# Three PSUM banks re-dealt, half-width projections and an earlier transpose in the first phase of a two-layer kernel

## The reference

```python
x1 = layernorm(x)                                    # folded with the next line into one scale and shift
z = rmsnorm(x1, pre_norm_w) @ in_proj_w.T            # 256 -> 768 channels
z_pre = causal_depthwise_conv(z, short_w, taps=3) + short_b
x2, x1, v = split(z_pre, 3)                          # 256 channels each
xv = x1 * v
y = (long_conv(xv, h) + xv * D_skip) * x2            # h from 16 poles a channel
...                                                  # out projection, gated MLP, layernorm; then an FFN layer
```

## Time and profile before

| | |
|---|---|
| median of 3 runs | 1097.38 us (1095.71 to 1097.52) |
| the profiled execution | 1095.71 us, span 1093.9 us |
| phase A | 0 to about 189 us of the span |
| PE busy | 97% of the span |
| DVE, ACT, POOL busy | 80%, 66%, 27% |
| granted TensorE clock | 0.998 of full speed |

### The profile page before, as it was taken

The page is one execution under the profiler, slowest core; times in us unless marked ns, Lnnn a source line. Parts: engine busy times, 40 slices in busy tenths (PEclk is TensorE's granted clock), DMA queues, the critical chain, the costliest instruction groups (busy, mean ns, idle before and its releaser), DMA issues.

```text
span 1093.9 us, 25039 instructions
## 1 busy us (share of the span) xinstructions
PE 1063.1 (97%) x9016; PEld 1007.7 (92%) x9016; DVE 879.1 (80%) x2313; ACT 720.8 (66%) x1613; POOL 298.7 (27%) x577
## 2 busy tenths in 40 slices
PE   8899999999999999999999999989999999999996
PEld 7777787778999999999999999989999999999996
DVE  7999998763788877888888777898888888877874
ACT  7878887664565666666666666665666666666553
POOL 6677784620001111112111111121112111111111
PEclk9999999999999999999999999999999999999999
DMA  3338988984642333333333333443333333333100
GB/s 127 117 126 229 270 229 219 400 312 59 147 73 40 59 60 49 59 49 50 52 55 63 56 59 49 109 105 50 50 59 49 51 53 57 65 59 49 31 11 30
DMA packets 113051, 104.93 MB, mean 96 GB/s; under 512 B 7600, under 2 KB 103792, under 8 KB 112672
## 3 DMA queue, kind: packets, MB, share of 16 engines
q1 hardware_dynamic: 111696, 100.77, 42.1%
q0 software_dynamic: 736, 2.51, 0.7%
q10 hardware_dynamic: 496, 0.05, 0.0%
HBM read 77.84 MB, written 32.80 MB: 101 GB/s over the span
## 4 chain that ended last, share of the span: by engine, by line
PE 63%; DVE 7%; issue 4%; POOL 1%; ACT 1%; DMA 0%; ACTq 0%; SPq 0%; DVEq 0%; POOLq 0%
PE ps_ring L1464 33%; PE ps_w L1464 14%; PE ps_m L1464 9%; PE ps_o L1464 4%; PE ps_rt L1479 2%; DVE base L1318 1%; POOL sc L1082 1%; DVE bn L1222 1%; PE ps_m L1529 1%; DVE prod L1265 0%; PE ps_w L1474 0%; DMA base<-in_w 0%; DVE ht_l L1234 0%; DVE pt_l L1234 0%; DVE x L1436 0%
## 5 line engine op out<-in xcount | busy, mean ns | idle before, releaser
L1082 POOL TENSOR_TENSOR sc<-sc,neg_half 128x2 f32<-128x2 f32 x128 | 95.5, 746 | 690.6 <-DVE sc L1417 407.8
L1142 ACT ACTIVATE gate<-ps_ring 128x256 f32<-128x256 f32 x192 | 73.0, 381 | 127.4 <-PE ps_ring L1464 126.6
L1163 ACT ACTIVATE hid<-ps_ring,b1s 128x256 f32<-128x256 f32 x256 | 112.4, 484 | 29.4 <-PE ps_ring L1464 9.3
L1464 PE MATMUL ps_ring<-mt_h,wl_h 128*128 128x256 f32 x640 | 125.8, 278 | 2.4 <-DVE prod L1265 1.3
L1464 PE MATMUL ps_ring<-mt_l,wl_h 128*128 128x256 f32 x640 | 125.7, 278 | 2.2 <-DVE mt_l L1234 2.2
L1464 PE MATMUL ps_ring<-mt_h,wl_l 128*128 128x256 f32 x640 | 125.0, 277 | 0.0
L1234 DVE TENSOR_TENSOR ht_l<-hid,ht_h 128x256 fp32r<-128x256 f32 x256 | 103.1, 423 | 16.0 <-ACT ht_h L1167 10.0
L1464 PE MATMUL ps_ring<-xt_h,we_h 128*128 128x256 f32 x512 | 103.2, 283 | 2.8 <-DVE prod L1265 2.4
L1265 DVE TENSOR_TENSOR prod<-ps_ring,gate 128x256 f32<-128x256 f32 x192 | 80.7, 420 | 24.9 <-ACT gate L1142 20.6
L1464 PEld LDWEIGHTS ps_ring<-mt_h,wl_h 128*128 128x128 f32 x640 | 96.6, 188 | 3.9 <-ACT mt_h L1211 2.2
L1464 PE MATMUL ps_ring<-xt_h,we_l 128*128 128x256 f32 x512 | 99.9, 276 | 0.0
(11 more groups left out here) (186 smaller groups left out, 2746.6 us busy)
## 6 DMA issues: line engine op xcount, KB each, us to landing
toep_scratch<-taps_scratch SPq DMA_DIRECT2D x30, 512.0 KB, 7.7
toep<-toep_scratch SPq DMA_DIRECT2D x30, 512.0 KB, 9.9
xa<-in_x SPq DMA_DIRECT2D x16, 512.0 KB, 5.0
x_scratch<-x2c SPq DMA_DIRECT2D x16, 512.0 KB, 3.7
x2s<-x_scratch SPq DMA_DIRECT2D x32, 256.0 KB, 6.9
xa_c<-in_x SPq DMA_DIRECT2D x32, 256.0 KB, 2.7
xb_c<-in_x SPq DMA_DIRECT2D x32, 256.0 KB, 2.7
out<-frow SPq DMA_DIRECT2D x32, 256.0 KB, 2.9
```

Source lines behind the costliest of these rows:

```text
L1082: nc.gpsimd.tensor_tensor(sc[:, to], sc[:, to], neg_half[:, 0, 0:CC], ALU.pow).then_inc(S[done], 1)
L1142: nc.scalar.activation(gate[rows_of, m % 2], ring[m % RING][rows_of, 0], ACT.Gelu_apprx_tanh).then_inc(S["gate_done"], 1)
L1163: nc.scalar.activation(hid[:, m % HIDS], block_of, ACT.Gelu, bias=b1s[:, m:m + 1]).then_inc(S["hid_done"], 1)
L1464: mm = nc.tensor.matmul(out, lhs(a, kk), rhs(b, kk), start=(j == 0), stop=(closed and j == len(todo) - 1))
```

## The change

- The PSUM banks are dealt anew: one bank `ps_t` for transposed rows where there were two, and five slots of `ps_z` where there were four. In unit 0 the second half goes to `ps_x0`.
- `turn_rows(n+1, 0)` moves from behind position 1 to behind position 0. Each `turn_rows` waits for the `turned_low` just before it. `turned_high` and `turned_low` of half 0 move to position 0, and DVE's `measure` calls to 1, 2, 4, 5.
- `norm_rows` does one chunk at each of the positions 2, 3, 4 and 5.
- `project` writes each bank in two halves of 256 columns, with twelve matmuls where there were six.
- At the second sequence's start ScalarE writes the bias, as for unit 0, and no longer GpSimd.

```diff
-    OVER, SLOTS, XBUFS = TAPS - 1, 4, 3
+    HALF, OVER, SLOTS, XBUFS = TA // 2, TAPS - 1, 5, 3
-    NORMED = {2: (0,), 4: (1,), 5: (2, 3)}
...
-        ps_t = [ps(ctx, f"ps_t{b}", [P, TA]) for b in range(KB)]
+        ps_t = ps(ctx, "ps_t", [P, TA])
...
+        def turned_bank(u, b):
+
+            return ps_x[0][:].rearrange("p c t -> p (c t)") if (u, b) == (0, 1) else ps_t[:]
...
             def carry(u, j):
-                over = pair[:, :, TA:]
-                if opens(u + 1):
-                    biases = sbias[:, KB:].rearrange("p (a k) -> p k a", k=KB)[:, j]
-                    over = biases.unsqueeze(2).broadcast_to([P, KB, OVER])
-                nc.gpsimd.tensor_copy(pair[:, :, 0:OVER], over).then_inc(S["carried"], 1)
+                nc.gpsimd.tensor_copy(pair[:, :, 0:OVER], pair[:, :, TA:]).then_inc(S["carried"], 1)
...
             def first_tap(u, i):
-                if u == 0:
+                if opens(u):
                     nc.scalar.activation(sums(m, u)[:, 0:OVER], zero[:], ACT.Identity, scale=1.0,
...
         def _(act):
-                    if i in (1, 3) and valid(n + 1, UA):
+                    if i in (0, 3) and valid(n + 1, UA):
                         turned_high(n + 1, i // 3)
                     if i in (1, 3) and valid(n - 1, UA):
                         gate_rows(n - 1, i // 2)
-                    if i in NORMED and valid(n + 2, UA):
-                        norm_rows(n + 2, NORMED[i])
+                    if i >= 2 and valid(n + 2, UA):
+                        norm_rows(n + 2, (i - 2,))
...
         def _(dve):
-                        if n == 0:
-                            dve.wait_ge(S["opened"], i + 1)
+                        if opens(n):
+                            dve.wait_ge(S["opened"], ZB * (n * B // UA) + i + 1)
...
-                    if i in (1, 3):
+                    if i in (0, 3):
                         if valid(n + 1, UA):
                             turned_low(n + 1, i // 3)
                     elif valid(n + 3, UA):
-                        measure(n + 3, i // 2 if i < 3 else i - 2)
+                        measure(n + 3, i - 1 if i < 3 else i - 2)
...
         def _(pe):
             def turn_rows(u, b):
                 if u > 0:
-                    pe.wait_ge(S["zl_done"], KB * (u - 1) + b + 1)
+                    pe.wait_ge(S["zl_done"], KB * u + b)
...
             def project(u, i):
-                passes = [(w, r, k) for w, r in ((0, 0), (1, 0), (0, 1)) for k in range(KB)]
-                for j, (w, r, k) in enumerate(passes):
-                    mm = nc.tensor.matmul(slot(b)[:], win_r[w][:, k, m * P:(m + 1) * P], zt[r][:, u % 2, k],
-                                          start=(j == 0), stop=(j == len(passes) - 1))
+                for a in range(2):
+                    cols = slice(a * HALF, (a + 1) * HALF)
+                    passes = [(w, r, k) for w, r in ((0, 0), (1, 0), (0, 1)) for k in range(KB)]
+                    for j, (w, r, k) in enumerate(passes):
+                        mm = nc.tensor.matmul(slot(b)[:, cols], win_r[w][:, k, m * P:(m + 1) * P],
+                                              zt[r][:, u % 2, k, cols], start=(j == 0),
+                                              stop=(j == len(passes) - 1))
                 mm.then_inc(S["z_mm"], 1)
...
-                    if i == 1 and valid(n + 1, UA):
+                    if i == 0 and valid(n + 1, UA):
                         turn_rows(n + 1, 0)
```

More of the change, by code:

```diff
@@ L359, in carry_x2 @@
                 wait(pool, x2_out[1 - u % 2], 16 * ((u + 1) // 2))
-                over = x2c[:, u % 2, :, TA:]
-                if opens(u + 1):
-                    over = sbias[:, 0:KB].unsqueeze(2).broadcast_to([P, KB, OVER])
-                nc.gpsimd.tensor_copy(x2c[:, 1 - u % 2, :, 0:OVER], over).then_inc(S["x2_carried"], 1)
+                nc.gpsimd.tensor_copy(x2c[:, 1 - u % 2, :, 0:OVER], x2c[:, u % 2, :, TA:]
+                                      ).then_inc(S["x2_carried"], 1)
             scan_consts()
@@ L411, in turned_high @@
                 wait(act, S["z_mm"], ZB * (u - 1))
-                nc.scalar.activation(zt[0][:, u % 2, b], ps_t[b][:], ACT.Copy).then_inc(S["zh_done"], 1)
+                nc.scalar.activation(zt[0][:, u % 2, b], turned_bank(u, b), ACT.Copy).then_inc(S["zh_done"], 1)
             def first_tap(u, i):
@@ L495, in turned_low @@
                 high = zt[0][:, u % 2, b]
-                nc.vector.tensor_tensor(zt[1][:, u % 2, b], ps_t[b][:], high.bitcast(F32), ALU.subtract
+                nc.vector.tensor_tensor(zt[1][:, u % 2, b], turned_bank(u, b), high.bitcast(F32), ALU.subtract
                                         ).then_inc(S["zl_done"], 1)
@@ L559, in turn_rows @@
                 if u > 0:
-                    pe.wait_ge(S["zl_done"], KB * (u - 1) + b + 1)
+                    pe.wait_ge(S["zl_done"], KB * u + b)
                 for c in range(CA):
-                    mm = nc.tensor.transpose(ps_t[b][:, c * P:(c + 1) * P], zn[:, u % 2, c, b * P:(b + 1) * P], ident[:])
+                    mm = nc.tensor.transpose(turned_bank(u, b)[:, c * P:(c + 1) * P], zn[:, u % 2, c, b * P:(b + 1) * P], ident[:])
                 mm.then_inc(S["zt_done"], 1)
@@ L567, in turn_gated @@
                 wait(pe, S["xs_done"], KB * (u - 1) + j + 1)
+                if u == 0:
+                    pe.wait_ge(S["zl_done"], KB)
                 for c in range(CA):
@@ L589, in keep_running @@
                     nc.tensor.transpose(dst, ident[:], ident[:])
-            spare, last_spare = ps_z[SLOTS - 1][:, 0:P], ps_t[0][:, 0:P]
+            spare, last_spare = ps_z[SLOTS - 1][:, 0:P], ps_t[:, 0:P]
             keep_running(spare, 16)
```

## The result

The changed kernel is slower: median 1103.82 us (1101.49 to 1105.3, 6 runs) against 1096.18 (1095.71 to 1097.52, 6 runs) of the kernel before beside it. The ratio is 1.0066, 95% interval 1.0053 to 1.008, so about 7.2 us more, with 5.8 to 8.8 in the interval. The forecast was 3.9 more. The profiled execution took 1102.86 us, span 1101.1; that of before, 1095.71 us, was the fastest of its six.

The account below looks back on a forecast made before the run. Steady phase A steps were taken as bound by loops through several engines, not TensorE alone. 2.59 us for steps 4 to 13 plus 1.33 for the tail made 3.92 more: 1099.6 us, or 1101.3 on the median; range 1098.0 to 1104.0.

Parts of the forecast that it names:

- The third loop, 10.54: Phase A: ScalarE's block 3 to last row chunk, moved turn, projections, back to block 3; sets the step at 10.54 us.
- Loops one and two, 10.25 before: Phase A: loops through ScalarE, DVE and GpSimd, over one step and, via `x_tap`, two; both bind at 10.25 us a step.
- Order within changes, the set of instructions does not: 5.12: Phase A: ScalarE from block 3's first tap to the end of the last row chunk stays 5.12 us.
- Steps 4 to 13, 2.59 more: Phase A, block 3 of step 4 to step 13: nine steps of 10.54 plus 0.57 for biases, 2.59 us more.
- Steps 0 to 3: nothing: Phase A's first steps, block 3 11.83 us apart with DVE never idle: 0 added.
- The tail, 1.33 more: End of phase A: a later turn with one projection more behind it, 1.10, plus 0.23 for splits: 1.33 us more.
- Phase A in all, 3.92: Whole of phase A: 2.59 and 1.33 together, 3.92 us more.
- Phases B and C are unchanged: Phases B and C begin behind a barrier of all engines: no change.
- Banks, faster: Rival, phase A: five slots let TensorE run ahead, its 5.7 us of waits go; 3.7 us less, 1093.7; chance 0.07.
- The hidden turn: Rival, phase A: TensorE waits once at the moved turn, steps stay 10.25; 1.9 us more, 1099.3; chance 0.18.
- DVE as the bound, 10.76: Rival, phase A: the chunk's 0.51 us ahead of `x_tap` adds to each step; 5.9 us more, 1103.3; chance 0.09.
- Half banks that cost a start each: Rival, phase A: 0.07 us for every projection; 1.9 us above the forecast, 1103.2; chance 0.06.

Follow-up runs that it names:

- a_pool_first: Changed kernel with GpSimd's add of x2's last tap behind the scales, measures earlier, loads of x ahead; ratio 1.0076 to the kernel before.
- b_norm: Kernel before with one row chunk at each of positions 2 to 5, nothing else; ratio 1.0011 to the kernel before.
- a_turn_back: Changed kernel with half 0's turn, its two readers and DVE's measures back at their old positions; ratio 1.0043 to the kernel before.
- a_full_width: Changed kernel with 512-column projections again; ratio 1.0038 to the kernel before.
- pool_first: Kernel before with GpSimd's add of x2's last tap behind the scales, measures earlier, loads of x ahead; ratio 1.0029 to the kernel before.
- b_turn: Kernel before with only half 0's turn, its readers and first measure moved up behind the first projection; ratio 1.0046 to the kernel before.
- a_split64: Changed kernel with only the first 64 of 96 projections in halves; ratio 1.0048 to the kernel before.
- b_split32: Kernel before with only the first 32 of 96 projections in two halves of 256 columns; ratio 1.0017 to the kernel before.
- b_shift: Kernel before with 36 more filler transposes at the end of TensorE's phase A; ratio 1.0027 to the kernel before.
- b_split: Kernel before with only the half-width projections added; ratio 1.0025 to the kernel before.
- b_split64: Kernel before with only the first 64 of 96 projections in two halves of 256 columns; ratio 0.9995 to the kernel before.

## Why the prediction came out as it did

The direction was right and the mechanism in phase A was right, by its own terms; the whole came out at about 7.2 us where 3.9 were forecast, because one step of it failed. That the time, 1103.82, lies within the range of 1098.0 to 1104.0 is luck: the upper end was set by two rivals (1103.3 and 1103.2) that did not happen, and what filled the range in their place was a loss in phase C that the prediction had at nothing.

- *The third loop, 10.54.* Right in its path and nearly so in its size. Measured 10.62 with each term in its place; a_pool_first shows that GpSimd's loops don't bind, b_norm and a_turn_back that without this loop the steps are 10.48, as loop two was to give (10.50 forecast). The mis-sized term is the splits: 0.06 in the loop was forecast, and the rows show 2.96 - 2.87 and 1.51 - 1.47, 0.13 together. Their spacing is a part of it: from 179.62 to 184.12, 38 matmuls of 256 columns take 0.1184 us each,

```profile
179.62 0.40 PE L582 MATMUL ps_z<-zt_h,win_h 128*128 128x256 f32 x2
...
184.12 0.40 PE L582 MATMUL ps_z<-zt_h,win_l 128*128 128x256 f32 x2
```

  so a pair costs 0.0040 more than one of 0.2328, which is 0.07 for 18. In the steady step, 24 of them from 139.94 to 142.90 are 0.123 apart with the first one's start in it. Over nine steps the miss is 0.6 us. Weight loads are hidden: 18 more of them in the loop cost 0.12 us together (10.62 against a_full_width's 10.50). The 3.9 us a step that exposed loads would cost, an estimate worked out from the Trainium skill, TensorE: Matmul & The Clock Gate, section on LDWEIGHTS, are nowhere in the trace; nor is its 107 ns for a load, the rows of the trace having 189 ns for one of `ps_z`.
- *Loops one and two, 10.25 before.* Their last terms (7.37 and 8.59) were worked out as what is missing to the next 10.25, so their sums had to come out, and that they bind was argued only. b_norm bears loop two out: a chunk in it gives 10.48. For loop one no run does; pool_first took the add out of it, but put it ahead of a carry that ScalarE then waits for.
- *Order within changes, the set of instructions does not: 5.12.* The number was right (5.13), the reason too weak. b_turn has the same set and 5.42, because two chunks stand behind the wait for block 4. The term is a path, and an order can put a wait of ScalarE's inside it.
- *Steps 4 to 13, 2.59 more.* Block 3 went from 70.16 to 166.20, 96.04 in place of 92.84: 3.20 more. The slack of before was swallowed as assumed: the steps into 8 and 9 are 10.95 and 10.80, 0.51 over the pace, where 0.57 was forecast for the biases, and before's own long step of 10.76 is not there on top. b_turn, which has the third loop's pace and no new biases, has no long step at all (10.78 and 10.79 there), so the 0.51 is the biases'.
- *Steps 0 to 3: nothing.* Block 3 of step 4 came 0.45 us earlier than before, so the sum was 0.45 too high here, about what varies without an edit.
- *The tail, 1.33 more.* From block 3 of step 13 to phase B: 193.60 - 166.20 = 27.40, before 189.39 - 163.45 = 25.94. That is 1.46 more.
- *Phase A in all, 3.92.* Measured -0.45 + 3.20 + 1.46 = 4.21.
- *Phases B and C are unchanged.* This is the step that failed: it was put at nothing because the phases begin behind a barrier, and 3.0 of the 7.2 us lie there. The text named it as what would make the prediction wrong, and gave it no price. 1152 more instructions are an estimated 72 KB more to fetch, which moves every later fetch by 4.5 packets of 16 KB, and one then met the 16 KB write at the seam: 2.1 us in the trace (1.4 by the later issue of `base`, 0.7 by its slower landing), and 2.0 in the timed ratios when a_split64 moved it away again. Phase B is not constant either: from its start to its end the changed kernel was 0.35 us faster than before, b_split32 1.7 slower.
- *What is left* is 7.2 - 4.2 - 2.1 = 0.9 us. In the trace 0.8 of it lie between 375 and 405 us, as a slightly lower rate of matmuls (265 of them in 30.8 us against 30.0, mean 280 ns against 276). Eleven of the fourteen traces have it; before, b_turn and pool_first don't, so it goes with no edit. Nine traces, but neither before nor the changed kernel, lose another 0.7 in the same way about 100 us behind the seam. The timed ratios leave 1.3 us of a_split64 (5.3 against 4.0) and 1.4 of a_full_width (4.2 against 2.8) above phase A's part, and nothing of b_norm and b_shift. Whether there is a further small cost that is none of these stays open; the intervals are 1.3 us wide to each side.

The rivals. Banks, faster: out, steps 0 to 3 did not get shorter by more than varies anyway, and the waits for xv turned into waits for `zn`; what the banks do by themselves was not measured. The hidden turn: out, the steps went to 10.62. DVE as the bound, 10.76: out, since b_norm, with the chunk at position 3 alone, has 10.48. Half banks that cost a start each: out, full-width projections shorten phase A by 1.38 us, not 2.5 or more, and b_split lengthens it by 0.44.

## What to carry over

Write out each closed loop with its terms, and when an instruction is moved, ask which loop it joins; the cost of two moves is that of the longest loop with both in it, and a move that costs when alone can pay beside another. A loop is shortened only if all loops of nearly its length are: pool_first took 11 us of waiting away in one place and found 5 in the next. Count instructions as traffic: an edit that only adds some can move fetches onto a small transfer that someone waits for, hundreds of us later; so compare the round trips of such transfers before a phase is called unchanged, and vary the number of added instructions before the edit itself is blamed. A loop's last term has to be read from rows like the others; worked out as the rest of the step, it makes any loop fit.

## What the hardware showed that I had not expected

- A fetch of instructions, one packet of 16 KB on queue 8 of the DMA, beside a 16 KB write to DRAM made that write's round trip 2.59 to 2.93 us at the seam and 2.11 to 2.60 at the start of phase C in five kernels; without it, it was 1.43 to 1.46 us at both places in nine. In the changed kernel 30 of the write's 32 packets start as early as before, and two only when the instruction packet is through (1.72 us behind the issue, the packet's end at 1.73). What makes up the other half of the longer round trip no run shows.
- The packets of the smaller instruction queue, 14, say nothing on this: in b_split64 and before they had ended 0.4 us ahead of the write's issue.
- One instruction of TensorE takes an estimated 64 bytes of that traffic (768 more made three packets more, 384 one, 1152 four).
- A half-width projection costs only 0.004 to 0.007 us for each pair of 256-column matmuls, with twice as many weight loads, all hidden.
- TensorE's granted clock was 0.50 for 3.4 us behind the longer wait at the seam in the changed kernel, and for as long in b_shift, whose wait there (1.0 us) was not longer than before and where no time was lost by it.
